# Exponentials on VectorE from the bits of a fixed-point score, with six strips in even heads; the product of the feed-forward layer a head later; a last head without row tiles

## The reference

```python
xn = layernorm(x)
q, k, v = xn @ Wq.T, xn @ Wk.T, xn @ Wv.T     # q: 4 groups x 8 heads x 16, k and v: 8 heads x 16
scores = einsum('bsqhd,bthd->bqhst', q, k) * 0.25
a_dot  = einsum('bqhst,bthd->bsqhd', softmax(scores), v)
sigma  = elu(q);  a_mem = sigma @ memory / (sigma @ memory_norm)
x = x + a_dot * (1 - w) + a_mem * w           # w = sigmoid(memory_weight)
x = x + (float8(clip(layernorm(x) / s)) * s) @ (weight * weight_scale).T
```

## Time and profile before

| | |
|---|---|
| median of 3 runs | 2017.57 us (2016.67 to 2018.4) |
| the profiled execution | 2018.72 us, its span 2017.0 us |
| ScalarE | 1876.7 us busy, 93% |
| TensorE matmul | 1736.2 us, 86% |
| VectorE | 1529.7 us, 76% |
| GpSimd | 99.5 us, 5% |
| ACT line 825 | 1892 instructions, mean 1121 ns |

### The profile page before, as it was taken

How to read it: one execution, slowest core, us unless ns; L and a number is a source line. 1 busy time by engine, 2 the same in 40 slices (tenths; PEclk the granted TensorE clock), 3 DMA queues, 4 the chain that set the end, 5 groups by cost and what they waited for, 6 DMA issues and landing times.

```text
span 2017.0 us, 77616 instructions
## 1 busy us (share of the span) xinstructions
PE 1736.2 (86%) x35884; PEld 664.5 (33%) x35892; DVE 1529.7 (76%) x1746; ACT 1876.7 (93%) x2100; POOL 99.5 (5%) x148
## 2 busy tenths in 40 slices
PE   8997788888888888888888888888888888888887
PEld 7883222222222222222222222222222222222225
DVE  7664687778777788778777788777877778877856
ACT  5555899999999999999999999999999999999996
POOL 5540000000000000000000000000000000000000
PEclk9998899999999999999999999999999999999999
DMA  6563111111122211212111211121111211121111
GB/s 230 198 199 104 40 39 50 50 42 51 37 53 53 74 40 45 53 56 59 40 50 53 74 48 36 53 73 43 48 40 53 74 53 39 46 74 45 49 39 45
DMA packets 131500, 128.37 MB, mean 64 GB/s; under 512 B 30518, under 2 KB 106726, under 8 KB 131174
## 3 DMA queue, kind: packets, MB, share of 16 engines
q1 hardware_dynamic: 130166, 121.55, 20.7%
q10 hardware_dynamic: 1008, 1.84, 0.3%
HBM read 87.36 MB, written 32.24 MB: 59 GB/s over the span
## 4 chain that ended last, share of the span: by engine, by line
ACT 64%; PE 19%; DVE 12%; issue 3%; DMA 1%; POOL 1%; SPq 0%; ACTq 0%; DVEq 0%; POOLq 0%
ACT pool L825 64%; PE ps L904 6%; PE ps L989 5%; PE ps L1105 5%; DVE late L1540 3%; DVE v_tiles L1546 3%; DVE late L1532 2%; DVE late L1537 2%; PE ps L1144 2%; PE ps L1203 1%; DVE y_out L1649 1%; PE ps L877 1%; DVE late L1544 0%; PE ps L1188 0%; DMA resid<-in_x 0%
## 5 line engine op out<-in xcount | busy, mean ns | idle before, releaser
L825 ACT ACTIVATE pool<-ps 128x1024 f32<-128x1024 f32 x1892 | 1752.6, 1121 | 44.9 <-PE ps L989 39.6
L1105 PE MATMUL ps<-pool,v_st 64*32 64x512 f32 x16128 | 1063.5, 593 | 11.4 <-issue 8.0
L989 PE MATMUL ps<-q_st,k_st 51*32 51x512 f16 x16128 | 770.4, 383 | 248.7 <-ACT pool L825 219.1
L989 PEld LDWEIGHTS ps<-q_st,k_st 51*32 51x32 f16 x16128 | 228.8, 90 | 1098.2 <-ACT pool L825 841.8
L1105 PEld LDWEIGHTS ps<-pool,v_st 64*32 64x32 f32 x16128 | 289.1, 106 | 134.4 <-issue 49.7
L1532 DVE TENSOR_SCALAR late<-ps 128x1024 f32<-128x1024 f32 x124 | 151.7, 1224 | 171.1 <-PE ps L989 171.1
L1562 DVE STREAM_TRANSPOSE by_token<-ps 128x512 f32<-128x512 f32 x126 | 82.5, 693 | 123.2 <-PE ps L1105 123.2
L1556 DVE SCALAR_TENSOR_TENSOR pool<-late 128x2048 f32<-128x2048 f32 x62 | 142.1, 2292 | 11.8 <-PE ps L1105 9.8
L1540 DVE SCALAR_TENSOR_TENSOR late<-late 128x2048 f32<-128x2048 f32 x62 | 142.1, 2292 | 2.1
L1553 DVE SCALAR_TENSOR_TENSOR late<-late,v_tiles 128x2048 f32<-128x2048 f32 x62 | 142.1, 2292 | 2.1
L1551 DVE SCALAR_TENSOR_TENSOR late<-v_tiles 128x2048 f32<-128x2048 f32 x62 | 141.8, 2286 | 1.2
(11 more groups left out here) (169 smaller groups left out, 1011.9 us busy)
## 6 DMA issues: line engine op xcount, KB each, us to landing
q_st<-q_aug SPq DMA_DIRECT2D x128, 128.0 KB
k_st<-k_aug SPq DMA_DIRECT2D x128, 128.0 KB
v_st<-v_aug SPq DMA_DIRECT2D x64, 256.0 KB, 3.0
sigma_kept<-y_out SPq DMA_DIRECT2D x32, 256.0 KB, 2.0
q_aug<-parts SPq DMA_DIRECT2D x32, 256.0 KB, 2.7
q_st<-q_aug SPq DMA_DIRECT2D x128, 64.0 KB
k_st<-k_aug SPq DMA_DIRECT2D x128, 64.0 KB
wqT<-sigma_kept SPq DMA_DIRECT2D x32, 256.0 KB, 3.0
```

The costliest lines, as they stand in the source:

```text
L825: act.activation(held[:, half_u * 2 * CH:half_u * 2 * CH + 2 * CH], sc[slot_of("exp", unit)].rearrange("p a b -> p (a b)"), ACT.Exp, scale ...
L989: last = pe.matmul(dst[VW * c:VW * c + VW, x, :], k_st[RT * x:RT * x + AUG, par, keys:keys + VW], q_st[RT * x:RT * x + AUG, par, q * CH:q ...
L1105: last = pe.matmul(acc[r][VW * c:VW * c + VW, :].rearrange("v (i s) -> v i s", s=VW), v_st[rows, par, j, :], by_place[rows, c, :, :], star ...
```

## The change

**Bits.** The strips' exponentials are formed in another way. The first instruction reads the slot, multiplies by -2^23/`OCTAVE` and converts to an int32, a fixed-point number. Its low 23 bits (`bitwise_and`, `bitwise_or`) give a fraction, its upper bits (`bitwise_and`, `bitwise_xor`) the power of two. Three more steps on the fraction make the polynomial: four `scalar_tensor_tensor` and two `tensor_scalar` a chain in place of five and two. The polynomial has no leading factor, so that all results are larger by a common one; ScalarE's exponentials get the same factor by a bias e^`LIFT`, for which each `activation` now names a 128 x 1 tile, `lift`.

**A third strip unit.** Even heads from 2 to 62 give a further unit (the second half of key tile 14) to VectorE; ScalarE has 29 units there. It is made in the odd head before at a = 22, the other two at a = 8 and 9 there. It has a chain of its own (`late_extra_strips`), and its tile is weighed in two halves.

**Moved.** The feed-forward product goes from a = 19 of an odd head to a = 2 of the even head after it, and `ffn_out` to the front of VectorE's head. `probs_place` shifts the ring by one place, so that head 0's last tile no longer uses `late_probs`. VectorE's wait for the stored v goes from ahead of head 0 into `late_end(1)`, and that end no longer waits for head 0's weighing; SyncE's wait for the guard goes behind the last v's store.

**Last head.** Its operands are loaded once and not twice, with GpSimd clearing `q_st` ahead of it (and `k_st` at the start of the kernel); the matmuls take all 128 rows. Tile t uses accumulator t % 2 alone, and `add_last_tile` has one transpose and no addition of halves.

```diff
-LATE_AT = (11, 12)
-WEIGHT_TURN_AT = 20
-PRODUCT_AT = 19
-LAST_PRODUCT_AT = 6
+LATE_AT = ((11, 12), (8, 9, 22))
+WEIGHT_TURN_AT = 15
+PRODUCT_AT = 2
+LAST_PRODUCT_AT = 1
+def late_units(n):
+    if not 0 < n < LAST_HEAD:
+        return 0
+    return LATE + (n % 2 == 0)
...
+    return 2 * ST - late_units(n)
...
+def product_tile(n):
+    tile = n // 2 - FIRST_PRODUCT_PAIR - 1
+    return tile if n % 2 == 0 and tile >= 0 else None
...
+            sp.wait_ge(keys_cleared, 1)
...
-            sp.wait_ge(guard_stored, 16 * NG)
...
             store_v(NG - 1, 1)
+            sp.wait_ge(guard_stored, 16 * NG)
...
+            pool_e.memset(k_st[:, :, :].rearrange("p a s -> p (a s)").bitcast(F32), 0.0).then_inc(keys_cleared, 1)
+            pool_e.memset(lift[:, :], LIFT).then_inc(ones_set, 1)
...
+            pool_e.wait_ge(scores_ready, EXP_BASE[LAST_HEAD - 1])
+            pool_e.memset(q_st[:, 1, :].bitcast(F32), 0.0).then_inc(last_cleared, 1)
...
-                                   sc[slot_of("exp", unit)].rearrange("p a b -> p (a b)"), ACT.Exp, scale=EXP_UNIT / SCORE_UNIT)\
+                                   sc[slot_of("exp", unit)].rearrange("p a b -> p (a b)"), ACT.Exp, bias=lift[:, :],
+                                   scale=EXP_UNIT / SCORE_UNIT)\
...
+                if late_units(n) > LATE and j == EXTRA_TILE:
+                    half_places = QG * TPC // 2
+                    weigh(n, j, held[:, 0:2 * CH], slice(0, half_places))
+                    pe.wait_ge(late_extra_ready, n // 2)
+                    last = weigh(n, j, late_extra[:, :], slice(half_places, 2 * half_places), last_tile=last_tile)
...
-                        last = pe.matmul(sc[slot_of("exp", unit)][VW * c:VW * c + VW, x, :],
-                                         k_st[RT * x:RT * x + AUG, 1, keys:keys + VW], by_tile, start=True, stop=True,
-                                         tile_position=(RT * x, VW * c))
+                        last = pe.matmul(sc[slot_of("exp", unit)][VW * c:VW * c + VW, x, :], k_st[:, 1, keys:keys + VW], by_tile,
+                                         start=True, stop=True)
...
+            def take_late(n, x, place):
+                number = LATE_BASE[n] + x
+                dve.wait_ge(late_scores, number + 1)
+                dve.tensor_scalar(late_x[:, place * 2 * CH:(place + 1) * 2 * CH].bitcast(I32),
+                                  sc[slot_of("late", number)].rearrange("p a b -> p (a b)"),
+                                  -2.0 ** 23 / OCTAVE, LOWEST, ALU.mult, ALU.min).then_inc(late_taken, 1)
+
+            def chain_begin(step, width):
+                fixed, part = late_x[:, 0:width], late_z[:, 0:width]
+                dve.tensor_scalar(part.bitcast(I32), fixed.bitcast(I32), MANTISSA, QUARTER,
+                                  ALU.bitwise_and, ALU.bitwise_or).then_inc(late_step, 1)
+                dve.wait_ge(late_step, step + 1)
+                dve.tensor_scalar(fixed.bitcast(I32), fixed.bitcast(I32), EXPONENT, ONE,
+                                  ALU.bitwise_and, ALU.bitwise_xor).then_inc(late_step, 1)
+                dve.scalar_tensor_tensor(part, part, POWER[0], part, ALU.add, ALU.mult).then_inc(late_step, 1)
+
+            def chain_end(step, width, dst):
+                power, part, grown = late_x[:, 0:width], late_z[:, 0:width], late_y[:, 0:width]
+                dve.wait_ge(late_step, step + 3)
+                dve.scalar_tensor_tensor(grown, part, POWER[1], part, ALU.add, ALU.mult).then_inc(late_step, 1)
+                dve.wait_ge(late_step, step + 4)
+                dve.scalar_tensor_tensor(grown, grown, POWER[2], part, ALU.add, ALU.mult).then_inc(late_step, 1)
+                dve.wait_ge(late_step, step + 5)
+                return dve.scalar_tensor_tensor(dst, grown, POWER[3], power, ALU.add, ALU.mult)
...
             def late_end(n):
+                if n == 1:
+                    for par in range(2):
+                        dve.wait_ge(v_stored[par], 16 * (NG // 2 + 1))
+                else:
+                    dve.wait_ge(pv_done, late_weighed(n - 1))
...
+            def late_extra_strips(n):
+                step = (chains_before(n) + 1) * CHAIN_STEPS
+                dve.wait_ge(late_ready, n)
+                take_late(n, LATE, 0)
+                dve.wait_ge(late_taken, LATE_BASE[n] + LATE + 1)
+                chain_begin(step, 2 * CH)
+                chain_end(step, 2 * CH, late_extra[:, :]).then_inc(late_extra_ready, 1)
...
-                for r in range(ROW_TILES):
-                    last = dve.transpose(last_by_token[:, r, t, :, :].rearrange("p q v -> p (q v)"), acc[r][:, 0:QG * VW])
-                last.then_inc(acc_read, 1)
+                tile = last_by_token[:, t, :, :]
+                dve.transpose(tile.rearrange("p q v -> p (q v)"), acc[t % 2][:, 0:QG * VW]).then_inc(acc_read, 1)
...
             def head(n):
                 g, h = divmod(n, HEADS)
+                if product_tile(n) is not None:
+                    ffn_out(*divmod(product_tile(n), TPC))
                 if n > 0:
                     add_head(n - 1)
...
-            for par in range(2):
-                dve.wait_ge(v_stored[par], 16 * (NG // 2 + 1))
             for n in range(LAST_HEAD):
                 head(n)
```

More of the change, by code:

```diff
@@ L89, in slot_turns @@
     for a in range(exp_units(n)):
-        if a in LATE_AT and has_late(n + 1):
-            turns.append(("late", LATE * n + LATE_AT.index(a)))
+        if a in late_at(n):
+            turns.append(("late", LATE_BASE[n + 1] + late_at(n).index(a)))
         if n == LAST_HEAD:
@@ L95, in slot_turns @@
         elif n % 2 == 0:
+            if a == PRODUCT_AT and product_tile(n) is not None:
+                turns.append(("product", product_tile(n)))
             if a == MEMORY_AT:
                 turns.append(("memory", n // 2))
[L98 to L103, removed]
+        elif n // 2 == WEIGHT_PAIR and a == WEIGHT_TURN_AT:
+            turns.append(("weight", 0))
         turns.append(("exp", EXP_BASE[n] + a))
     return turns
+LATE_BASE = [sum(late_units(m) for m in range(n)) for n in range(LAST_HEAD + 2)]
 EXP_BASE = [sum(exp_units(m) for m in range(n)) for n in range(LAST_HEAD + 2)]
@@ L498, in v_dst, with load_qk @@
                 return v_aug[bass.ds(c, 1), :, :, :].rearrange("a h p w -> p (a h) w")
-            def load_qk(n, g, h, par, done):
+            def load_qk(n, g, h, par, done, copies=ROW_TILES):
                 head = slice(h * DH, h * DH + DH)
@@ L504, in load_qk @@
                 keys = k_parts[bass.ds((g // CPB) * CPB, CPB), head, :, :]
-                for r in range(0, P, RT):
+                for r in range(0, copies * RT, RT):
                     sp.dma_start(q_st[r:r + PARTS * DH, par, :], high.unsqueeze(1).to_broadcast([DH, PARTS, QG * CH])).then_inc(done, 16)
@@ L521, in v_src, with load_guard @@
                 return v_aug[bass.ds(b4, CPB), h, :, :].rearrange("c p w -> p c w")
-            def load_guard(g, h, par, done):
-                for r in range(0, P, RT):
+            def load_guard(g, h, par, done, copies=ROW_TILES):
+                for r in range(0, copies * RT, RT):
                     sp.dma_start(q_st[r + ROWS:r + AUG, par, :].rearrange("i (o s) -> i o s", o=QG),
@@ L704, in _, with rstd_of_tiles @@
             bound_roots(1)
[L706 to L709, removed]
+            def rstd_of_tiles(first, end):
+                with pool_e.Fori(first, end) as i:
+                    pool_e.wait_ge(f_eps, i + 1)
+                    pool_e.tensor_tensor(rstd[:, 0, 0:1], var_eps[:, 0:1], minus_half[:, 0:1], ALU.pow).then_inc(f_rstd, 1)
+                    pool_e.wait_ge(f_rstd, i + 1)
+            rstd_of_tiles(0, (NG - 1) * TPC - 1)
+            pool_e.wait_ge(scores_ready, EXP_BASE[LAST_HEAD - 1])
+            pool_e.wait_ge(f_rstd, (NG - 1) * TPC - 1)
+            pool_e.memset(q_st[:, 1, :].bitcast(F32), 0.0).then_inc(last_cleared, 1)
+            pool_e.wait_ge(last_cleared, 1)
+            rstd_of_tiles((NG - 1) * TPC - 1, NT)
             pool_e.wait_ge(xq_ready, NT)
@@ L832, in _ @@
                 act.wait_ge(scores_ready, unit + 1)
[L833 to L834 removed]
+                act.activation(last_probs[:, last_place(v), :, :, :].rearrange("p x q s -> p (x q s)"),
+                               sc[slot_of("exp", unit)].rearrange("p a b -> p (a b)"), ACT.Exp, bias=lift[:, :],
+                               scale=EXP_UNIT / SCORE_UNIT)\
                     .then_inc(probs_ready, 1)
@@ L1104, in weigh @@
                         rows = slice(RT * r, RT * r + RT)
-                        last = pe.matmul(acc[r][VW * c:VW * c + VW, :].rearrange("v (i s) -> v i s", s=VW),
-                                         v_st[rows, par, j, :], by_place[rows, c, :, :], start=first, stop=last_tile,
+                        last = pe.matmul(acc[r][VW * c:VW * c + VW, :].rearrange("v (i s) -> v i s", s=VW)[:, places, :],
```

(9 more changed lines are left out.)

174 lines of the change are left out of this document (87 added, 87 removed).

## The result

The changed kernel takes 2108.75 us (median of 4 runs, 2107.3 to 2109.41), the kernel before 2017.63 beside it: a ratio of 1.045 (95% interval 1.043 to 1.047). The forecast was 2076 us, range 2020 to 2112. Its sign and its main cause hold; one cost, the bias tile's, was too small by some 15 us, and one saving, the waits in a pair, too large by some 18. One execution of experiment 4 took 9272 us at a mean granted clock of 0.165, for which the runs show no cause, and is left out of that experiment's figures.

A forecast was written before the change was run, and what follows sets the result against it. ScalarE's exponentials were taken to set the pace. From 2018.7 us: -28.5 + 140 - 29 - 18.6 - 5 - 0.5 = 2077.1, less 1.15 to the median: 2076 us, 2.9% slower, range 2020 to 2112.

The forecast's parts named there:

- The bias tile: Every ScalarE exponential pays for reading its bias from a tile: 0.074 us on 1893, 140 us more (121 to 172).
- Waits in a pair: ScalarE's waits per pair of heads fall from 1.15 to 0.1 us, covered by the slower pace: 29 us less.
- The third strip's slot: Odd heads, a = 22: VectorE reads the slot in time for unit 24, with 0.5 us to spare.
- Rival 3: VectorE late in odd heads, third strip's slot holds up unit 24, 0.8 us in 31 heads: 2101 us; chance 0.07.
- Fewer exponentials: 31 even heads give one unit more to VectorE, sparing ScalarE 31 x 0.921 = 28.5 us.
- Heads 0 and 1: Moved waits and the shifted ring remove ScalarE's stalls in the first two heads: 18.6 us less.
- Rival 4: The first stall is only moved, as SyncE's last store or VectorE still waits: 18.6 us back, 2095; chance 0.05.
- Last head: Fewer TensorE matmuls leave 1.0 us of ScalarE's 6.0 us of waits: 5 us less, and 0.5 in the tail.
- GpSimd's clearing: Clearing k_st at the start takes about 2 us within 9 us of idle time, so costs nothing; uncovered, 2 us.
- Rival 1: The tile's read is hidden behind the exponential ahead, the pace stays at 0.921 us: median 1968 us; chance 0.14.

The follow-up runs named there:

- experiment 4: The changed kernel, bias tile kept, with the feed-forward product at a = 1 of even heads in place of a = 2: 2106.3 us, ratio 1.044.
- run 1: The kernel before, with only its exponentials' bias read from a 128 x 1 tile of zeros: 2144.4 us, ratio 1.064.
- run 2: The changed kernel with the same bias as a constant in the instruction, not a tile: 2009.7 us, ratio 0.9963.
- run 10: Constant bias, memory product at a = 8, strips at 12 and 13, and 9 and 10, without the third strip unit: 1981.4 us, ratio 0.982.
- run 5: The changed kernel, bias tile kept, with the feed-forward product at a = 0 of even heads: 2091.7 us, ratio 1.037.
- Run 3: The changed kernel with constant bias and the three moved waits at the start put back: 2032.5 us, ratio 1.008.
- runs 7 and 9: The changed kernel, constant bias, later places: memory product a = 8, odd strips 9, 10, 25 (1972.5 us); also memory product 9, even strips 13, 14 (1968.4 us).

## Why the prediction was right, and where it was short

**The bias tile** set the sign, as forecast: run 1 shows it alone (128 us in the kernel before) and run 2 without it (99 us in the changed one). The one copy with a tile in the earlier trace rows was enough to see that its read isn't hidden. An exponential that stands alone lasts 1.11 us (at 177.35) and 1.02 before, as forecast. The size in the pace was short. I took a pace of 0.995 between 0.985, which started from the spacing of starts in an unbroken run, and 1.012. It is 1.003, the chain's 0.921 and 0.082 on it: 0.008 x 1893 = 15 us of the 33 that were missing. The low end rested on starts only. In the earlier trace rows they are 0.905 apart, but each exponential of the run also lasts a little longer than the one ahead (1.02 us grows to some 1.23), and TensorE waits for ends. The changed kernel's run of exponentials does the same. The 0.921 itself is not quite the pace either: 0.917 (run 10) is, and the surcharge against it is 0.086. That moves 0.004 a unit from the pace of before to the waits of before and leaves the sum as it is.

**Waits in a pair** is the step that failed. It said that the product at a = 2 is "covered to within 0.1" and the memory product, with "1.75 of 1.9", too. I counted TensorE's time and not the turn of the slot, and started the memory product's sum from a weighing that I took to be on time. Runs 4 and 5 show in its place a wait of 0.84 at unit 7, about 0.7 net in a head: the 27 even heads from 10 to 62, 18 us; run 5, which takes it out, is 17 us faster. That leaves 29 us less as some 11.

**The third strip's slot** was forecast to fit with 0.5 us to spare at the slow pace, and it does: 54 exponentials run on from unit 7 of head 16, past unit 24 of head 17. Only two of the 31 odd heads are longer, by 0.7 us each: head 7, with a wait of 0.33 at unit 24, and head 23, with one of 0.49 at unit 9. Rival 3 is out. VectorE's 47.8 us a pair are as summed up.

**Fewer exponentials**: 1861, as the diff says. In the changed kernel a spared one is worth 1.003.

**Heads 0 and 1**: both stalls gone, the clock from 184 us on at 1.00 where it had been at 0.50. The forecast was 18.6 us. At the slow pace the two heads last 65.2 us in place of 79.9; with the 62 x 0.082 = 5.1 us that the tile costs in them, that is 19.8. Run 3 gives 22.8 at the fast pace. Rival 4 is out.

**Last head**: its 32 exponentials take 32.07 us to the last one's start, so 33.07 with it, against 32 x 1.003 = 32.1: the 1.0 of waits that were left in the forecast. The row by stretches, and with it how full TensorE is:

```profile
2061.54:2093.61 32.07, 32.00 (x788) 18.96 (x776) 20.69 (x53) 31.34 (x33) 2.17 (x3) 1.00 0.10 36
```

**GpSimd's clearing** took 1.80 us in a gap of 10 us. In this execution the heads begin 1.5 us later than before (170.35 for 168.82); the shift is there at the first copies, at 11.2 us for 9.9. The clearing is not its cause: runs 7 and 9 have it too, and there the heads begin at 168.2 and 168.6. That part was not tried by itself.

**Rival 1** was out, but its condition, the pace of before, is what run 2 sets up, and there its 1968 us would have been wrong by 42. Even heads have 1.25 us of waits there and not the 0.3 that it had left (27 heads, 26 us), odd ones 0.3 more at the third strip (9 us), and the twelve long odd heads cost some 10 us more: 3.4 by late landings, 3.7 with the clock at 0.50, the rest in heads 7 and 61. Together that is about 42.

**Luck.** That 2108.75 lies in the range is in part luck. The room above 2076 was left for a dearer tile and for rival 3. The tile was dearer by 15 us; the other 18 came from a wait that the prediction held to be covered.

## What to carry to other kernels

A constant folded into an engine's instruction through a tile is not free where that engine sets the pace: here 0.08 us each, 1893 times, more than all that the change saved; ask first whether the same number can stand in the instruction. In a ring of slots an extra turn costs lead and not only time: look at which release each of the next turns waits for, and what stands behind that turn on the in-order engine. When work is moved to an engine that runs behind, place its hand-over where that engine gets to it: the same third strip was worth -6 us at one place and 25 at another. And look at the reader behind: the memory product's later place left even heads at 28.0 us until the strips behind it moved too, to 27.5.

## What was not expected of the hardware

With constants, 1024 columns have a start every 0.905 us but an end only every 0.917 or so over a run, so that durations grow from 1.02 to 1.36 us. With the tile the starts are 0.997 apart, the ends 1.005, and durations still grow. So what the tile's read costs in the pace depends on the measure: 0.092 by starts, 0.088 by ends, 0.086 over whole heads (1.003 against 0.917), and 0.082 against the chain's 0.921; one instruction's duration grows by 0.090. So the 0.082 is no sign that a part of the read is hidden. What holds the ends back was not tried.
